# First adapter of a two-layer block: one semaphore per weight, batch 0 first, batch 1's adapter placed among batch 0's projections

## The reference

```python
# adapter of batch b, r = index of its profile (128 hidden)
z = relu(x @ down_w[r] + down_b[r])
h = layernorm(x + z @ up_w[r] + up_b[r]) * ln_g[r] + ln_b[r]
# time mixing: hs is h moved on by one token
xx  = hs - h
xxx = h + xx * maa_x
m   = tanh(xxx @ maa_w1)                    # 4 groups of 32
xf  = h + xx * (maa_f + m_f @ maa_w2[f])     # f = w, k, v, r
r, k, v = xr @ W_r, xk @ W_k, xv @ W_v
w   = exp(-exp(decay + tanh(xw @ dw1) @ dw2))
```

## Time and profile before

| | us |
|---|---|
| three runs | 1887.28, 1888.35, 1889.16 |
| median of the runs | 1888.35 |
| span of the profiled execution, first to last instruction | 1886.9 |
| median of the runs less that span | 1.45 |
| TensorE busy in the span | 1806.0 (96%) |
| VectorE, ScalarE, GpSimd busy | 1075.7, 922.1, 559.0 |

### The profile page before, as it was taken

How to read it: one execution, slowest core, us unless ns; L and a number is a source line. 1 busy time by engine, 2 the same in 40 slices (tenths; PEclk the granted TensorE clock), 3 DMA queues, 4 the chain that set the end, 5 groups by cost and what they waited for, 6 DMA issues and landing times.

```text
span 1886.9 us, 41313 instructions
## 1 busy us (share of the span) xinstructions
PE 1806.0 (96%) x17140; PEld 1301.8 (69%) x17140; DVE 1075.7 (57%) x2315; ACT 922.1 (49%) x1693; POOL 559.0 (30%) x961
## 2 busy tenths in 40 slices
PE   5989999999999978999999999999999999999997
PEld 3466768675575745777777777766777777777775
DVE  4573754143323146888888788854555554445453
ACT  2204222203234214888888888863555544445522
POOL 1353130014311161212111112103554543455413
PEclk9889999989999989999999999999999999999999
DMA  6100000402435459610102111000000000010001
GB/s 187 25 1 24 4 1 1 139 27 86 134 123 167 123 156 205 110 45 21 41 21 75 63 28 34 22 2 23 2 2 2 2 2 2 2 30 2 2 0 45
DMA packets 89933, 93.55 MB, mean 50 GB/s; under 512 B 35267, under 2 KB 75139, under 8 KB 89603
## 3 DMA queue, kind: packets, MB, share of 16 engines
q1 hardware_dynamic: 83490, 79.12, 15.6%
q0 software_dynamic: 3456, 9.44, 1.9%
q10 hardware_dynamic: 2800, 2.34, 0.4%
HBM read 68.34 MB, written 23.07 MB: 48 GB/s over the span
## 4 chain that ended last, share of the span: by engine, by line
PE 89%; DVE 5%; DMA 2%; ACT 2%; issue 1%; POOL 1%; SPq 0%; POOLq 0%; DVEq 0%; ACTq 0%
PE PS L1776 13%; PE PS L1190 7%; PE PS L1790 7%; PE PS L1199 7%; PE PS L2115 6%; PE PS L1767 6%; PE PS L2193 5%; PE PS L2170 4%; PE PS L2120 3%; PE PS L2154 3%; PE PS L576 2%; PE PS L668 2%; PE PS L2200 2%; PE PS L2232 1%; PE PS L675 1%; PE PS L523 1%
## 5 line engine op out<-in xcount | busy, mean ns | idle before, releaser
L1949 DVE CUSTOM_DVE_ANT_0 arena<-PS,arena 128x1024 f32<-128x1024 f32 x256 | 311.9, 1219 | 62.1 <-PE PS L1767 58.5
L1870 ACT ACTIVATE arena<-arena 128x1024 f32<-128x1024 f32 x256 | 296.7, 1159 | 9.4 <-DVE arena L1949 9.1
L1776 PE MATMUL PS<-arena 128*128 128x128 f32 x2048 | 280.1, 280 | 2.7 <-issue 2.4
L1776 PEld LDWEIGHTS PS<-arena 128*128 128x128 f32 x2048 | 230.5, 142 | 63.3 <-issue 30.5
L2397 POOL TENSOR_SCALAR arena<-arena 128x384 f32<-128x384 f32 (+1 forms) x256 | 142.8, 569 | 252.0 <-DVE arena L2306 252.0
L2278 ACT ACTIVATE arena<-arena 128x385 f32<-128x385 f32 (+1 forms) x256 | 151.4, 593 | 128.6 <-DVE arena L2315 128.6
L1866 ACT COPY arena<-PS 128x512 f32<-128x512 f32 x298 | 169.9, 585 | 64.3 <-PE PS L1776 62.0
L1767 PE MATMUL PS<-arena 96*128 96x512 bf16 x512 | 154.7, 383 | 4.9 <-DVE arena L1949 3.8
L2315 DVE CUSTOM_DVE_ANT_0 arena<-PS,arena 128x384 f32<-128x384 f32 (+1 forms) x256 | 123.2, 537 | 52.3 <-PE PS L2157 39.9
L1956 DVE COPY arena<-PS 128x512 f32<-128x512 f32 x214 | 146.8, 686 | 4.8 <-PE PS L1776 4.6
L1190 PE MATMUL PS<-arena 128*128 128x512 f32 x320 | 139.9, 594 | 6.6 <-ACT arena L1318 5.9
(11 more groups left out here) (331 smaller groups left out, 3094.3 us busy)
## 6 DMA issues: line engine op xcount, KB each, us to landing
arena<-in_L_ffn_W SPq DMA_DIRECT2D x16, 1024.0 KB, 7.2
arena<-prior SPq DMA_DIRECT2D x16, 512.0 KB, 4.1
parts<-arena SPq DMA_DIRECT2D x24, 256.0 KB, 4.8
arena<-parts SPq DMA_DIRECT2D x96, 64.0 KB, 2.9
arena<-parts SPq DMA_DIRECT2D x48, 128.0 KB, 9.8
prior<-arena SPq DMA_DIRECT2D x4, 1024.0 KB, 6.2
ye<-arena SPq DMA_DIRECT2D x7, 512.0 KB, 3.0
ya<-arena SPq DMA_DIRECT2D x7, 512.0 KB, 4.9
```

The source lines that it names most:

```text
L1776: h = e.transpose(PS[:, i, P * j:P * j + P], Sb[z % 3][:, 512 * g + P * j:512 * g + P * j + P], ident)
L1870: e.activation(Sb[z % 3], Sb[z % 3], ACT.Exp, bias=mr[:, z % 4:z % 4 + 1], scale=-1.0).then_inc(s_exp, 1)
L1949: e.tensor_tensor_reduce(Sb[z % 3], ps, Ab[m % 2], 1.0, 3e38, ALU.add, ALU.min, mr[:, z % 4:z % 4 + 1]).then_inc(s_ttr, 1)
```

## The change

1. The adapter's semaphores are split: `down_w` has one, `small` and `up_w` share one, `up_b` has one. Each user waits for what it reads. `small` is issued ahead of `up_w`.
2. ScalarE's queue issues the identity (with a semaphore of its own), x of batch 0, the other four constants, x of batch 1. TensorE waits for the identity alone; VectorE waits for the other constants ahead of `mix`.
3. TensorE begins with 22 bf16 products of a constant, as soon as GpSimd has written it. Their result isn't read.
4. Batch 1's workspace lies on space that only batch 1's tensors use later, so `phase_b` may begin on batch 0 alone.
5. `phase_a` runs batch 0's adapter only. Its T pieces go by token halves. Batch 1's z, y, norm and T stand in ORDER among batch 0's projections.
6. `mix(b)` works by halves of 512 tokens, each after the T pieces of its half.

```diff
+    def pieces(name, b):
+        if name == "z":
+            return [("z", n, b) for n in range(2)]
+        if name == "y":
+            return [("y", t, b) for t in range(TB_)]
+        return [("T", c, g, b) for g in range(2) for c in range(2)]
...
-        e.dma_start(s.wu[0:k], ...).then_inc(s_w[b], 16)
-        e.dma_start(s.small, ...).then_inc(s_w[b], 16)
+        e.dma_start(s.small, ...).then_inc(s_wu[b], 16)
+        e.dma_start(s.wu[0:k], ...).then_inc(s_wu[b], 16)
...
-            w.wait_ge(s_w[b], 64)
+            w.wait_ge(s_bub[b], 16)
             ready_x(w, b)
...
+            if b + c + g == 0:
+                unread(e, K, i, 10)
...
+    FIRST = [s for name in "zyT" for s in ad.pieces(name, 0)]
...
     def pe(e, w):
-        w.wait_ge(K.s_const, 80)
-        ad.pe(e, w)
+        w.wait_ge(K.s_ones, 1)
+        ones = K.onesm.bitcast(BF16)
+        for _ in range(22):
+            e.matmul(PS[:, 7, :]..., ones[:, 0:P], ones..., start=True, stop=True)
+        w.wait_ge(K.s_ident, 16)
+        for s in FIRST:
+            ad.pe(e, w, s)
...
-    ORDER = project(0)[:5] + [("G", 1)] + project(0)[5:] + [("mx", 1)] + in_turn(pairs(0), project(1))
+    def adapt(name, lo, hi):
+        return [("ad", 1, s) for s in ad.pieces(name, 1)[lo:hi]]
+
+    ORDER = project(0)[:3] + adapt("z", 0, 2) + project(0)[3:5] + [("G", 1)] + project(0)[5:7] + adapt("y", 0, 4) + project(0)[7:9] + adapt("y", 4, 8) + [("norm", 1)]
+    ORDER += project(0)[9:10] + adapt("T", 0, 4) + project(0)[10:] + [("mx", 1)] + in_turn(pairs(0), project(1))
...
-            e.tensor_tensor(xx[:, :, 1:S], hT[:, :, 0:S - 1], hT[:, :, 1:S], ALU.subtract).then_inc(s_bx, 1)
-            e.tensor_scalar(xx[:, :, 0:1], hT[:, :, 0:1], -1.0, None, ALU.mult).then_inc(s_bx, 1)
-            for c in range(2):
-                e.scalar_tensor_tensor(out=xxx[:, c], ...).then_inc(s_bx, 1)
+            w.wait_ge(K.s_const, 64)
+            for n in range(2):
+                w.wait_ge(*ad.done(b, n))
+                s0, s1 = 512 * n, 512 * n + 512
+                e.tensor_tensor(xx[:, :, s0 + 1 - n:s1], ..., ALU.subtract).then_inc(s_bx, 1)
+                if not n:
+                    e.tensor_scalar(xx[:, :, 0:1], hT[:, :, 0:1], -1.0, None, ALU.mult).then_inc(s_bx, 1)
+                w.wait_ge(s_bx, 7 * b + 3 * n + 2)
+                for c in range(2):
+                    e.scalar_tensor_tensor(out=xxx[:, c, s0:s1], ...).then_inc(s_bx, 1)
```

More of the change, by code:

```diff
@@ new lines, in pe @@
+    def pe(e, w, s):
+        b, key = s[-1], (tag,) + s
+        i = ring.bank(key)
+        w.wait_ge(*ring.free(key))
+        if s[0] == "z":
+            n = s[1]
+            w.wait_ge(s_wd[b], 16)
+            ready(w, b)
+            for c in range(2):
+                h = e.matmul(PS[0:k, i, :], ws[b].wd[:, c, :], hT[b][:, c, 512 * n:512 * n + 512], start=c == 0, stop=c == 1)
+        elif s[0] == "y":
+            t = s[1]
+            w.wait_ge(s_wu[b], 32)
+            w.wait_ge(*ring.emptied((tag, "z", t // 4, b)))
+            h = e.matmul(PS[:, i, 0:D], ws[b].zT[0:k, P * t:P * t + P], ws[b].wu[0:k, :], start=True, stop=True)
+        else:
+            _, c, g, _ = s
+            if b + c + g == 0:
+                unread(e, K, i, 10)
+            w.wait_ge(s_norm, 8 * b + 4 * g + 4)
+            for j in range(4):
+                h = e.transpose(PS[:, i, P * j:P * j + P], ws[b].y[:, 4 * g + j, P * c:P * c + P], K.ident)
+        h.then_inc(ring.sem, 1)
@@ new lines, in act_std, with dve, stats @@
+    def act_std(e, w, b):
+        w.wait_ge(s_var, b + 1)
+        e.activation(ws[b].st[:, 72:80], ws[b].st[:, 64:72], ACT.Sqrt).then_inc(s_std, 1)
+    n_st = {}
+    def dve(e, w, own, s):
+        _, t, b = s
+        q, key = ws[b], (tag,) + s
+        def stats(x):
+            w.wait_ge(*ring.emptied((tag, "y", x, b)))
+            n_st[b, x] = own.step(e.bn_stats(q.st[:, 6 * x:6 * x + 6], q.y[:, x, :]))
+        w.wait_ge(s_xb, 4 * b + t // 2 + 1)
+        w.wait_ge(*ring.filled(key))
+        e.tensor_tensor(q.y[:, t, :], PS[:, ring.bank(key), 0:D], q.xb[:, t, :], ALU.add).then_inc(ring.into(key), 1)
+        if t:
+            stats(t - 1)
+        if t == TB_ - 1:
+            stats(t)
@@ new lines, in dve_norm @@
+    def dve_norm(e, w, own, b):
+        s = ws[b]
+        for t in range(TB_):
+            own.after(n_st[b, t])
+            n = own.step(e.bn_aggr(s.mv[:, t, :], s.st[:, 6 * t:6 * t + 6]))
+        own.after(n)
+        e.tensor_scalar(s.st[:, 64:72], s.mv[:, :, 1], 1e-5, None, ALU.add).then_inc(s_var, 1)
+        w.wait_ge(s_std, b + 1)
+        n = own.step(e.reciprocal(s.st[:, 80:88], s.st[:, 72:80]))
+        own.after(n)
+        for t in range(TB_):
+            e.tensor_scalar(s.y[:, t, :], s.y[:, t, :], s.mv[:, t, 0:1], s.st[:, 80 + t:81 + t], ALU.subtract, ALU.mult).then_inc(s_norm, 1)
@@ L722, in act @@
         for name, b, *s in ORDER:
-            if name == "m":
+            if name == "ad" and s[0][0] != "y":
+                ad.act(e, w, *s)
+            elif name == "norm":
+                ad.act_std(e, w, b)
+            elif name == "m":
                 if b:
@@ L730, in act @@
                 dst = {"k": kT, "r": rT}[name][b]
-                for j in range(B):
-                    w.wait_ge(*ad.done(j))
+                w.wait_ge(*ad.done(b))
                 for n, c in NC:
@@ L885, in dve @@
         for name, b, *s in ORDER:
-            if name == "mx" or (name == "m" and b == 0):
+            if name == "ad" and s[0][0] == "y":
+                ad.dve(e, w, own, *s)
+            elif name == "norm":
+                ad.dve_norm(e, w, own, b)
+            elif name == "mx" or (name == "m" and b == 0):
                 mix(b)
```

142 lines of the change are left out of this document (53 added, 89 removed).

## The result

The changed kernel takes 1871.88 us (median of 5 runs, 1871.57 to 1873.43) against 1887.75 us for the kernel before (5 runs, 1883.98 to 1889.16): 15.9 us less, a ratio of 0.9916 with a 95% interval of 0.9892 to 0.9939. The forecast was 1870.9 us in a range of 1865 to 1877. The span of the profiled execution went from 1886.9 to 1870.1 us, 16.8 us less.

A forecast was written before the change was run, and what follows sets the result against it. Bound: a transfer wait at the start, serial work until x at 53.66 us, then TensorE from 69.6 us to the first D. Terms -9.0 - 11.3 - 3.4 + 6.2 = -17.5 from 1888.35 gave 1870.9 us, range 1865 to 1877.

The forecast's parts named there:

- behind D: Stretch after the first D: 4 us allowed either way, 1867 or 1875 us; chance 0.06.
- Step 1: Program start to VectorE's first adapter addition: at 14.8 us instead of 23.80, 9.0 us earlier.
- z finds the full clock: At the start: the 22 constant products cost nothing and z then runs at full clock.
- Step 2: First y to VectorE's start on x: 18.6 us instead of 29.9, 11.3 us shorter, x starting near 33.4.
- unchanged: First y to first transpose: 8.1 us, as in the kernel before.
- Step 3: x, gate and d1: 3.4 us shorter, the gate's 36 records taking about 4.3 us at full clock.
- the rival in which the clock is low before the gate: Clock falls before the gate and stays low through it: no gain from x to d1, 1874.3 us; chance 0.13.
- The rival in which the clock stays low: Clock stays low through the gate: no gain from x to d1, 1874.3 us; chance 0.13.
- Step 4: d2 to first D: 6.2 us longer, batch 1's y (3.56) and transposes (2.64) where TensorE is the bound.
- if x starts after 38: Test at VectorE's start on x: the forecast is wrong if it comes after 38 us; 33.4 was expected.
- The two more table loads: ScalarE, square root and tanh for batch 1: costed at nothing; 5.3 us worse by the skill if nothing covered them.
- x delayed the weights: Rival at the start: x's transfer delays batch 0's weights, a gain of 4.8 not 9.0 us, 1875.1 us; chance 0.11.

The follow-up runs named there:

- second profile: The changed kernel profiled and timed once more with no edit (after_again): 1872.16 us, ratio 0.9889 to the kernel before.
- e_xb: Changed kernel with GpSimd's x + up_b sums of batch 1 moved behind its last x piece of batch 0: 1869.76 us, ratio 0.9903.
- best2_again: Changed kernel with the four edits of e_warm, e_table, e_xb and e_swap, run a second time: 1871.75 us, ratio 0.9877.
- v_wholemix: Changed kernel with mix for all 1024 tokens at once, after the last T piece: 1877.26 us, ratio 0.9934.
- e_warm: Changed kernel with 32 instead of 22 products of a constant at the start: 1878.49 us, ratio 0.9919.
- best2: Changed kernel with the four edits of e_warm, e_table, e_xb and e_swap, first run: 1872.53 us, ratio 0.9899.
- after_again: The changed kernel once more, no edit, for a second profile: 1872.16 us, ratio 0.9889.
- e_table: Changed kernel with a single-column ScalarE activation ahead of the first relu, so relu's table loads during the transfers: 1872.58 us.
- e_swap: Changed kernel with the gate between batch 0's second and third x piece and batch 1's z behind the last: 1877.52 us, ratio 0.9927.

## Why the prediction held

The total was right, within 1.0 us, and that closeness is luck. The direction and the places of the three gains and of the cost were right, their sizes were not: all three gains were put too high and the one cost too. At D the sum was 4.6 to 5.9 us short of the forecast, and the difference was made up where I had written nothing into the sum.

| step | forecast | first profile | second |
|---|---|---|---|
| 1, to the first addition | -9.0 | -7.5 | -6.1 |
| 2, to x | -11.3 | -8.2 | -9.2 |
| 3, to d2 | -3.4 | -1.1 | -2.8 |
| 4, d2 to D | +6.2 | +5.2 | +5.2 |
| sum at D | -17.5 | -11.6 | -12.9 |
| behind D | 0 | -5.2 | -2.3 |

*Step 1.* The side on which I had set the end, up_b and x on GpSimd, was about right: GpSimd began at 13.13, where I had 13.5. The other side was the later one. "xT and down_w land at about 10.2": down_w landed at 11.2, and z started at 11.32. From there I had 4.2 us and it took 4.95, since the first addition came 0.78 us after y's start rather than 0.45 and the handovers to relu and from it, 0.4 us together, were left out. In the second profile z ran mostly at half clock, 1.4 us more: "z finds the full clock" was not sure at all.

*Step 2.* The term that failed is the 8.1 us from the first y to the first transpose, which I had called "unchanged". It measured 10.2 (9.1 in the second profile), and e_xb shows the cause, GpSimd's sums for batch 1 beside the norm: without them 8.1 again (25.56 - 17.47). I had allowed 0.3 us for it; in the trace before these sums ran beside additions that read PSUM, which they did not slow, and the norm came after them. The earlier start moved the norm onto them. The first two T pieces and their evictions took 2.9 us, not 2.2, as the clock was at half from 23.4 to 30.3 us (2.24 in best2_again, where they ran at full clock at first), and from mix to x it was 8.6 us, not 8.0.

*Step 3.* "I expect the clock to fall again during the gate", and so it did, one to three us into it. But the gate's 36 records took 6.7 us in the first profile and not 4.3, and 5.5 in the second; only in the four profiles in which the clock fell after the first 32 records had run, or with the last of them, did these take 3.7 to 3.8 us (v_wholemix, e_warm, best2, best2_again). As a sign for the rival in which the clock is low before the gate I had counted 12 us of the gate's own products at half clock; in the earlier trace rows the gate has 7.8 of them, and the rest is d1. The rival in which the clock stays low came to pass for most of the gate in the first profile. That batch 1's z costs nothing where it stands was right: the third x piece began 7.4 us after the first, as before.

*Step 4.* The transposes take 0.11 us each at full clock (1.74 us for 16), not 0.165: in the row that I took the earlier trace rows the four start 0.11 to 0.17 us apart as well, and its 0.66 us takes in the last one's own 0.27. The y were right, 3.5 us against 3.56. VectorE was in time; it waited 1.67 us for D, where I had said 2.

*Behind D* I had said 4 us either way and written nothing into the sum, and called the forecast wrong if the distance from the first D to the end differed by more than 3 us from before: it was 1784.9 and became 1779.7. By that test the forecast fell in the first profile (in the second the distance was 1782.6). By the test "if x starts after 38" it held by a hair in the first, 37.95, and fell in the second, 38.32. What filled the gap behind D was a clock that rose at 126 us, 35.5 behind D, where it had risen 44 behind D before; by after_again, where it rose 41.9 behind D, that moment varies with the same kernel. So of the 15.2 to 16.8 us in the two spans, 11.6 to 12.9 are shown at D and come from the change; of the rest, the part as far as kE (4.2 and 1.1 us) goes with the clock, and 1 us behind kE is open.

The two more table loads cost nothing, as forecast. The square root's, at 73.82, was over at 75.1, 2.4 us before its activation at 77.55, and tanh's, at 91.09, was over at 92.37, 2.0 us before its activation at 94.39. What the Trainium skill, ScalarE: Activation LUTs, "What ACT_TABLE_LOAD costs", says of a drain of 1.38 us beside the load doesn't show here either: the load at 15.94 begins right behind the relu that ends at 15.93. x delayed the weights less than its rival had it: up_b landed at 12.75 us, as before (12.79), while xT landed 7.6 us after its issue, not 6.6, and down_w 8.3, not 5.6, with x beside them. That agrees in kind with what the Trainium skill, DMA: Bandwidth & Descriptors, "Issuing engines are not separate DMA queues", says, that transfers of different queues share the 16 engines and interleave.

## What to carry to other kernels

When a serial head is shortened, look at what the other engines run at a time that transfers set, not the chain: here GpSimd's sums stood still at 21.6 to 25.9 us and the chain moved onto them, so that in eight profiles, with first additions from 15.06 to 17.87 us, the first transpose came 9.1 to 10.9 us behind the addition and not 8.1. Products like the gate's, in which the clock fell each time, may stand better where another engine is the bound, with other work behind them before TensorE is the bound again: from x to d2 it was 19.3, 21.4 and 19.7 us in three such profiles, against 21.1 to 22.7 in the seven with the gate behind x and no products ahead of it. And where a total was forecast well, compare it by landmarks with two profiles of the same kernel; a few us far behind the change can be the clock alone.

## What the hardware showed that was not expected

- A TENSOR_SCALAR of 128x256 from SBUF to SBUF on VectorE takes 0.40 us, and up to 1.18 us beside a GpSimd addition, and then ends 0.15 us behind it; VectorE's additions that read PSUM kept their 0.41 us beside the same work (15.06 to 19.37 us in e_table, GpSimd busy from 13.07).
- In all 12 profiles of the changed order the gate began at full clock and the clock fell to 1.2 GHz before it had ended, though TensorE counted as busy, and it rose only during the products behind it (d1 or the unread ones behind it in the changed order, z in e_swap, best2 and best2_again).
- In the two profiles in which TensorE had done nothing (or one product) before z, the records give the granted clock as 1.00 there, yet z's records are 0.86 us apart at first and 0.43 later. At the very start of a program the spacing tells the clock, the record does not.
